# Routing the first two rounds of nodes beside the last edge groups of a graph layer

## What is computed

```python
ea = (s_src[:, src] + s_dst[:, dst]).T                  # attention score of each edge
m  = segment_max(ea, dst); ea = exp(ea - m[dst]); s = segment_sum(ea, dst)
x  = x + segment_sum(h[src] * (ea / s[dst]), dst) + mix(xn)
xf = layernorm(x)
probs = softmax(xf @ gate_w + gate_b); top2 = top_k(probs, 2)
out = x + sum over e of cw[:, e] * (gelu(xf @ W1[e] + b1[e]) @ W2[e] + b2[e])
```

## Time and profile before

| | before |
|---|---|
| runs, us | 3241.82, 3248.89, 3249.25 (median 3248.89) |
| span of the profiled execution, us | 3246.6 |
| instructions | 42100 |
| PE busy | 2642.4 us, 81% |
| POOL busy | 2234.9 us, 69% |
| DVE busy | 2010.3 us, 62% |
| ACT busy | 1549.7 us, 48% |

### The profile page before, as it was taken

One profiled execution on the slowest core, in us unless ns is written; L12 is line 12 of the kernel. 1 busy time (PEld: TensorE's weight loads), 2 busy tenths in 40 slices (PEclk: granted clock), 3 DMA queues, 4 the chain that ended last, 5 costly groups with the idle time before them and its releaser, 6 DMA issues.

```text
span 3246.6 us, 42100 instructions
## 1 busy us (share of the span) xinstructions
PE 2642.4 (81%) x11512; PEld 2052.3 (63%) x11512; DVE 2010.3 (62%) x5442; ACT 1549.7 (48%) x3382; POOL 2234.9 (69%) x2193
## 2 busy tenths in 40 slices
PE   8657767888888888888888887566359999999998
PEld 6546655666666665666656656344247888778887
DVE  7446557667777676777767766677654555445422
ACT  5325544544555554555455554334234545545444
POOL 0277777777777777777777777776476767676554
PEclk9879988999999999999999998777569999999999
DMA  9797766566666666666566665565766676766663
GB/s 276 242 295 211 199 178 169 162 173 177 164 172 180 172 172 170 174 179 171 163 180 172 173 169 153 160 181 136 253 198 146 151 160 148 162 142 131 131 110 62
DMA packets 397637, 561.15 MB, mean 173 GB/s; under 512 B 71912, under 2 KB 317950, under 8 KB 397225
## 3 DMA queue, kind: packets, MB, share of 16 engines
q0 software_dynamic: 123696, 298.61, 36.3%
q1 hardware_dynamic: 196473, 170.69, 18.1%
...
## 4 chain that ended last, share of the span: by engine, by line
PE 65%; DMA 10%; ACT 8%; POOL 8%; issue 6%; DVE 2%; ACTq 0%; SPq 0%; POOLq 0%; DVEq 0%
PE bank L1314 21%; PE bank L2295 11%; PE bank L2308 10%; DMA rows<-table,srcix 9%; PE bank L1095 7%; POOL rows L1232 6%; PE bank L1084 5%; PE bank L1057 2%; PE bank L865 1%; PE bank L605 1%; PE bank L606 1%; ACT L1354 1%; PE bank L2284 1%; ACT xg L842 1%; PE bank L1296 1%
## 5 line engine op out<-in xcount | busy, mean ns | idle before, releaser
L1232 POOL DMA_INDIRECT rows<-table,srcix x1661 | 1600.3, 963 | 506.4 <-issue 354.2
L1314 PE MATMUL bank<-rows,onehot 128*128 128x272 f32 x3328 | 928.6, 426 | 57.4 <-ACT fout L1370 52.0
L1370 ACT ACTIVATE fout<-bank 128x272 f32<-128x272 f32 x1659 | 638.6, 397 | 574.7 <-PE bank L1314 525.3
L1314 PEld LDWEIGHTS bank<-rows,onehot 128*128 128x128 f32 x3328 | 666.5, 208 | 244.3 <-ACT fout L1370 78.7
L1463 DVE TENSOR_TENSOR rows<-rows,bank 128x1024 f32<-128x1024 f32 x416 | 484.0, 1213 | 173.2 <-ACT rows L1359 172.8
L2386 POOL DMA_INDIRECT out<-x_y,x_dest x203 | 325.0, 1601 | 233.2 <-DMA out<-x_y,x_dest 173.4
L2295 PE MATMUL bank<-x_int,x_w1c 128*128 128x256 f32 (+1 forms) x1696 | 379.7, 378 | 25.5 <-issue 22.2
L2308 PE MATMUL bank<-e_w,x_ht 128*128 x1624 | 370.5, 381 | 9.5 <-issue 7.0
L2295 PEld LDWEIGHTS bank<-x_int,x_w1c 128*128 128x128 f32 x1696 | 316.4, 194 | 77.4 <-issue 35.6
L2334 ACT ACTIVATE x_ht<-bank,x_b1c 128x256 f32<-128x256 f32 (+1 forms) x424 | 173.1, 462 | 394.4 <-PE bank L2295 392.9
L2308 PEld LDWEIGHTS bank<-e_w,x_ht 128*128 128x128 f32 x1624 | 300.2, 190 | 51.3 <-issue 14.8
...
## 6 DMA issues: line engine op xcount, KB each, us to landing
frag<-fout ACTq DMA_DIRECT2D x104, 544.0 KB
rows<-table,srcix POOLq DMA_INDIRECT x1661
...
x_b2c<-in_L_ffn_b SPq DMA_DIRECT2D x106, 128.0 KB, 3.5
...
```

The lines of the kernel that those rows point to most:

```text
L1232: p.indirect_dma_start(out=B.rows[b][:, j, :], out_offset=None, in_=B.table[:, :], in_offset=bass.IndirectOffsetOnAxis(ap=B.srcix[:, col:c ...
L1314: pe.matmul(B.banks[2 + c % 3][:, 0:ROW], B.onehot[k % 2][:, j, :], B.rows[k % NR][:, j, :], start=True, stop=True).then_inc(S.sum, 1)
L1370: a.activation(B.fout[k % 2][:, j, :], B.banks[2 + c % 3][:, 0:ROW], ACT.Copy).then_inc(S.ev, 1)
```

## The change

- Two rounds of routing (`FIRST`) join the chain of `Beside` on every engine, between the merge of the earlier windows and that of the last one. A table of call numbers, `schedule`, now says which step is due: MLP by group 90, three merge windows by the end of group 97, a new window of 48 chunks by the middle of group 100, 50 routing steps by the end of group 100, 190 by the end of group 101, all 240 by the end of group 102. A last window of 80 chunks comes after the groups.
- POOL gathers the node sums of rounds 0 and 1 (16 DMAs) ahead of the row gathers of group 103 (`first_fetches`, `FETCH_AT`), and scatters both rounds behind them, ahead of the second barrier.
- The order of sums and scores in the groups stays: only group 103 is `held`.
- The experts' weights are issued by SP in the last merge window, once the last sum is made (`expert_weights`). Zero rows, the biases and the nodes of rounds 2 and 3 come after the barrier (`later_sync`).
- Buffers move: the first two rounds' lie beside the edge stage's, and one small barrier of four engines (`freed`) precedes the 48-chunk window. `frag` has the node rows first and the chunks behind them.
- `paces` starts the tiles with no routing step ahead of them; round 2 is to be sent two parts of a tile ahead of its first use.

The core of the diff:

```diff
+def schedule():
+    routing = sum(round_steps(r) for r in range(FIRST_ROUNDS))
+    mlp = MIX_STEPS + MLP_STEPS
+    parts = mlp + BEFORE_STEPS
+    first = parts + PART_STEPS
+    return [(0, 0), (MIX_STEPS, MIX_STEPS), (MLP_END, mlp), (WHOLE_END, parts), (PART_FROM, parts + 1), (PART_END, first),
+            (FIRST_FROM - 1, first), (FIRST_FROM, first + 50), (FIRST_FROM + 4, first + 190), (FIRST_FROM + 7, first + 190),
+            (FIRST_FROM + 8, first + routing)]
...
+def first_fetches(p, S, B):
+    p.wait_ge(S.free, FREE)
+    p.wait_ge(S.a_zero, 32)
+    p.wait_ge(S.mg_out, 16 * (BEFORE + 1))
+    for b in range(2):
+        p.wait_ge(S.far[b], 16 * CB * ((SPLIT + 1 - b) // 2))
+    for r in range(FIRST_ROUNDS):
+        for i in range(R_TILES[r]):
+            fetch_sums(p, S, B, r, i)
...
 def edges_pool(p, S, B, groups):
     for k in groups:
         b = k % NR
+        if k == FETCH_AT:
+            first_fetches(p, S, B)
...
-    beside = Beside(mix_vector(v, vec, S, B), mlp_vector(v, vec, S, B), merge_vector(v, vec, S, B))
+    beside = Beside(mix_vector(v, vec, S, B), mlp_vector(v, vec, S, B), merge_vector(v, vec, S, B, WINDOWS[:-1]), first_vector(v, vec, S, B),
+                    route_vector(v, vec, S, B, FIRST), merge_vector(v, vec, S, B, WINDOWS[-1:]))
...
+def expert_weights(sp, S, B):
+    sp.wait_ge(S.sum, CB * GROUPS)
+    for e in range(EXPERTS):
+        sp.dma_start(B.w1[:, e, :, :], B.a["L0_ffn_W1"][e].rearrange("(k p) n -> p k n", p=P)).then_inc(S.x_w1, 16)
+    for e in range(EXPERTS):
+        sp.dma_start(B.w2[:, e * HT:(e + 1) * HT, :], B.a["L0_ffn_W2"][e].rearrange("(k p) n -> p k n", p=P)).then_inc(S.x_w, 16)
...
+def later_sync(sp, S, B):
+    sp.dma_start(B.b1[:, :, :], B.a["L0_ffn_b1"].rearrange("e (k p) -> p e k", p=P)).then_inc(S.x_b, 16)
+    sp.wait_ge(S.e_pad, 1)
+    sp.dma_start(sorted_rows(B.sorted_d[ZERO_ROWS:ZERO_ROWS + ET, :]), B.pl_zero[:, :, :]).then_inc(S.e_z, 16)
+    for r in (FIRST_ROUNDS, FIRST_ROUNDS + 1):
+        fetch_nodes(sp, S, B, r)
...
-    due = [(0, sum(round_steps(r) for r in range(FIRST_ROUNDS + 1)))]
-    due += [(order.index(r) - EARLY * (1 + (r == len(ROUNDS) - 1)), sent[r]) for r in range(FIRST_ROUNDS, len(ROUNDS))]
+    lead = lambda r: 2 if r == FIRST_ROUNDS else EARLY * (1 + (r == len(ROUNDS) - 1))
+    due = [(0, 0)] + [(order.index(r) - lead(r), sent[r]) for r in LATER]
...
     barrier(p, S, 1)
     ends_pool(p, S, B)
     edges_pool(p, S, B, range(GROUPS))
-    barrier(p, S, 2)
-    late(route_pool(p, S, B), experts_pool(p, S, B))
+    reach(p, S)
+    for _ in route_pool(p, S, B, FIRST):
+        pass
+    p.wait_ge(S.stage, MEET[2])
+    later_pool(p, S, B)
+    late(route_pool(p, S, B, LATER), experts_pool(p, S, B))
```

More of the change, by code:

```diff
@@ L197, with reach, freed @@
 MEET = {1: 5, 2: 10}
+FREE = 4
+def reach(e, S):
+    e.drain().then_inc(S.stage, 1)
 def barrier(e, S, i):
-    e.drain().then_inc(S.stage, 1)
+    reach(e, S)
     e.wait_ge(S.stage, MEET[i])
+def freed(e, S):
+    e.drain().then_inc(S.free, 1)
+    yield
+    e.wait_ge(S.free, FREE)
 def idle(steps):
@@ L1319, in edges_tensor @@
     for k in range(GROUPS):
-        more, early = k + 1 < GROUPS, k + 2 < GROUPS
+        more = k + 1 < GROUPS
+        early = more and not held(k + 1)
         if early:
@@ L1398, in edges_scalar @@
             a.dma_start(B.last_d[k * CB:(k + 1) * CB, :], B.fout[k % 2][P - 1:P, :, :]).then_inc(S.near[k % 2], 16)
-        if k + 3 < GROUPS:
+        if k + 2 < GROUPS and not held(k + 2):
+            if 4 * k + 4 == FIRST_FROM:
+                beside()
             copy_scores(k + 2)
-        beside()
-    for _ in beside.steps:
-        pass
+        if 4 * k + 4 != FIRST_FROM:
+            beside()
+    beside.rest()
     a.wait_ge(S.a_zero, 32)
@@ L1493, in edges_vector, with numbered, merge_sync @@
         beside()
-    for _ in beside.steps:
-        pass
+    beside.rest()
 COLUMNS = [(h * P, (h + 1) * P) for h in range(KD)] + [(D, D + GH)]
 BANK_H0, BANK_H1, BANK_T = 5, 6, 7
-def merge_sync(sp, S, B):
-    ends = B.frag[0:FAR].rearrange("(b c l) f -> l c b f", c=P, l=NEAR)[0]
-    lasts = B.last_d.rearrange("(b c) f -> c b f", c=P)
-    for w, (b0, m) in enumerate(WINDOWS):
+def numbered(windows):
+    return [(WINDOWS.index(w), *w) for w in windows]
+def merge_sync(sp, S, B, windows):
+    for w, c0, m, n in numbered(windows):
+        ends = B.frag[NEARS:FRAGS].rearrange("(b c l) f -> l c b f", c=P, l=NEAR)[0]
+        lasts = B.last_d.rearrange("(b c) f -> c b f", c=P)
+        b0, p0, upto, M = c0 // P, c0 % P, (c0 + m * n) // CB, B.merges[w]
+        first, last = M.first[w % 2], M.last[w % 2]
@@ L1523, in merge_sync @@
         yield from idle(MERGE_STEPS - 1)
-        if final:
-            sp.wait_ge(S.near[k % 2], 32 * (GROUPS // 2) - 16)
-        sp.wait_ge(S.mg_sum, 3 * (w + 1))
-        sp.dma_start(ends[:, b0:b0 + m, :], B.first[w % 2][:, 0:m, :]).then_inc(S.mg_out, 16)
+        if not final:
+            sp.wait_ge(S.mg_sum, 3 * (w + 1))
+            sp.dma_start(ends[p0:p0 + n, b0:b0 + m, :], first[0:n, 0:m, :]).then_inc(S.mg_out, 16)
         yield
-    sp.wait_ge(S.mg_out, 16 * len(WINDOWS))
-def merge_tensor(pe, S, B):
+    if windows[-1] == WINDOWS[-1]:
+        sp.wait_ge(S.mg_out, 16 * len(WINDOWS))
@@ L1533, in merge_tensor @@
+def merge_tensor(pe, S, B, windows):
     bk = B.banks
-    for w, (b0, m) in enumerate(WINDOWS):
-        last = B.last[w % 2]
+    for w, c0, m, n in numbered(windows):
+        M = B.merges[w]
+        last = M.last[w % 2]
+        if w == BEFORE:
+            yield from freed(pe, S)
         yield from idle(4)
@@ L1703 @@
 SPREAD = 3
-FIRST_ROUNDS = 2
 GATES = 2 * P
@@ L1928, in steps @@
         yield
-    for r in range(len(ROUNDS)):
+    for r in rounds:
         yield from marked(r, steps(r))
```

461 lines of the change are left out of this document (280 added, 181 removed).

## The result

The changed kernel takes 3271.11 us (median of 4 runs, 3265.14 to 3272.8) against 3248.76 for the kernel before on the same chip. Over all runs the ratio is 1.0073, 95% interval 1.0059 to 1.0088. It is slower by 0.7%, where I forecast no difference. The profiled execution has a span of 3269.8 us, against 3246.6: 23.2 us to be found.

The account below looks back on a forecast made before the run. POOL was taken to bound the edge stage, then a chain of small steps, and PE behind 2392. Span 3246.6 - 5.7 + 4.3 + 3 = 3248.2, taken as 3248 us; range 3228 to 3266.

Parts of the forecast that it names:

- last sum: End of the edge stage, tail set by DVE: last sum at 2340, 56 us later than before; bounds 2330 and 2350.
- barrier: After SP issues the 16 weight DMAs, all engines meet at 2360; bounds 2356 and 2379.5.
- tile 0's second product ends: Start of the experts: rows at 2381 plus 26.3 us give 2407.7, 5.7 us ahead of before.
- what is added behind it: Behind the experts' start: 4.3 us of round 2's gate, turning back, counts and table swap, plus 3 us waiting for tile 9.
- signs of being wrong: Last sum before 2330 or after 2350, barrier after 2366, repeated PE waits for x_in, or a loss before 2240.
- The rival by which the weights hold SP: Before the experts: weight issue takes 36.6 us, everybody meets at 2379.5; about 17 us slower, 3265; chance 14%.
- the overlap as such gives nothing: Last groups: no free DVE time, so beside means behind; this is the forecast, 3238 to 3258; chance 47%.
- a wait for tile 9: Among the first expert tiles: PE waits for tile 9's rows, first to need round 2's scatters; 3 us, bounds 0 and 12.
- ACT's table swap: Behind the experts' start: PE waits 2.4 us for ACT's table swap in each round; part of the 4.3 us added.
- theory C: From the experiments: ACT's eight normalizations of a round in one slot stall PE's first product 2.4 us; split four and four, none.
- once it passes some 40 us (six buffers of 7.35 us tiles) PE stands: Expert tiles: POOL's backlog grows as round 2's and 3's gathers move there; PE stands only past some 40 us.
- POOL becomes the bound: Expert tiles: POOL's backlog grows until PE stands; with tile 9 at 12 us, 3261, slower; chance 12%.

Follow-up runs that it names:

- the run with round 2 ahead of the tiles: Changed kernel with all 110 steps of round 2 again ahead of the first expert tile: ratio 1.0041 to the kernel before, span 3256.4 us.
- the changed kernel with every fourth step: Changed kernel with POOL's routing scatters and gathers every fourth step instead of every third: ratio 0.9986 to the kernel before, span 3235.6 us.
- the kernel before with every fourth step: Kernel before with POOL's routing scatters and gathers every fourth step instead of every third: ratio 0.9911, median 3214.15 us, span 3218.7.
- the kernel before held early: Kernel before with POOL held about 13 us ahead of tile 6's additions by six unread gathers: ratio 1.0043, span 3260.2 us.
- the one relieved of eight additions: Changed kernel without the second addition of tiles 3 to 10 (output incomplete): ratio 1.0036 to the kernel before, span 3254.6 us.

## Why the prediction was wrong, step by step

| step of the prediction | forecast | measured |
|---|---|---|
| node gathers, group 103's gathers end | 2262.9, 2279.2 | 2261.1, 2278.2 |
| last sum | 2340 | 2335.9 |
| issue of the weights | 17 to 20 us | 22.3 us |
| barrier | 2360 | 2361.5 |
| first tile turned | 2381 | 2384.0 |
| tile 0's second product ends | 2407.7 (-5.7) | 2408.4 (-4.9) |
| what is added behind it, to tile 12 | +7.3 | +14.1 |
| last tiles and backlog | 0 | +5.6, +8.1 |

**Right:** everything up to tile 0, within some 4 us at each step. For the last sum this was partly luck: from 2243 to 2335.9 DVE was busy for 65.9 us where I had added up 75.6, and idle for 27.0 where I had 18.5 (and 3 for the last pieces), 12.3 of it in one wait for gathered node sums. (2381 + 26.3 is 2407.3, not the 2407.7 that I wrote; it changes nothing.) None of my signs of being wrong showed, since none of them lay behind tile 0 but a wait for `x_in`. The rival by which the weights hold SP did not happen: they took 22.3 us, not 36.6. That the overlap as such gives nothing was right in kind, and the run with round 2 ahead of the tiles puts a number on it: +10 us.

**"What is added behind it", mis-sized:** I counted round 2's remaining PE work (4.3 us) and a wait for tile 9 (3 us). Tile 9 was never waited for. The waits came at rounds 3 and 4 (9.2 + 4.0 us), since the new table packs steps almost twice as densely; my text counts what round 2 adds and never asks what happens to the density of the rounds behind it. The order of PE at the start showed the changed steps, and `paces` could have been worked out. The 2.4 us a round that I put to ACT's table swap are the stalls of theory C: where the eight normalizations are split they are gone, with the swaps still there, and between the tiles 0 and 12 of the changed kernel there was none.

**The step that failed, on POOL:** "once it passes some 40 us (six buffers of 7.35 us tiles) PE stands". I read "mostly waits for its own additions (173 of 233 us idle)" as idle time, and asked only whether a backlog would stop PE. The chain of additions has a cycle of its own, 5.8 to 7.7 us a tile without scatters against PE's 7.35. A backlog is therefore worked off slowly or not at all, and what is left behind the last y is added to the span one to one (+8.1 us), long before any buffer is full. The limit was wrong as well: it is set by seven `x_dest` buffers claimed some two tiles ahead, about 30 us for full tiles, and in the half tiles (4.1 us each) 22 us of backlog stopped PE (5.6 us in all). The rival "POOL becomes the bound" had the right engine and 3261; its mechanism and place were not these.

**The range** (3228 to 3266) missed by 5 us, since both bounds of the POOL term were drawn from one wait, and none from the end.

**What stays open:** why the backlog of the changed kernel keeps to 21.5 to 21.9 us from tile 80 to 88 while the same chain gains 0.7 us a tile in the kernel before. The traces show more than my theory says. From tile 84 to 88, where no round is scattered, the backlog rests at one of three levels in five kernels, one PE tile (7.35 us) apart: at 6.8 to 7.1 us with round 2 ahead of the tiles and in the changed kernel with every fourth step, at 14.1 to 14.4 in the kernel before with every fourth step, at 21.5 to 21.9 in the changed kernel and in the kernel before held early. On a level the wait for the landing is 3.5 to 3.9 us, and POOL keeps PE's pace. The backlogs of the kernel before and of the one relieved of eight additions are between two levels at tile 84; their wait is 2.5 to 3.3 us, and they fall by up to 1.5 us a tile until they reach 6.8. So the landing seems to be slow when the additions start at a certain point of PE's tile, and how far a backlog is worked off depends on where it happens to stand. Behind tile 89 all of them leave their level again. SP issues its three loads of a tile (`x_in`, `x_b1c`, `x_b2c`) at that pace too; whether they are the reason was not tried.
